# One-hot iota and residual tiles in a PSUM bank of VectorE's own, loads of the MLP loop in mid-turn, and a gather ring of 16 in the second layer

## The chip, the cores and the metric

The kernel runs on one core of a Trainium2 chip. The metric is device time in microseconds (us) of one execution. The core's engines work side by side and meet at semaphores: PE (TensorE, matmuls and transposes), DVE (VectorE), ACT (ScalarE), POOL (GpSimd, which here mostly issues gathers) and SP (which issues DMAs and passes on their landings).

## What is computed

Three blocks on a graph of 6250 nodes with 256 features and 100000 edges sorted by target:

```python
xn = layernorm(x)
# two SAGE layers: mean over incoming edges of gathered rows, two matmuls each
h   = relu(mean(xn[src] -> dst) @ W1l.T + b1 + xn @ W1r.T)
gnn =      mean(h[src]  -> dst) @ W2l.T + b2 + h @ W2r.T
# linear attention and an MLP with two layer norms
q, k, v = split(xn @ Wqkv.T);  q, k = elu(q) + 1, elu(k) + 1
t   = (q @ (k.T @ v)) / (q . sum(k) + eps)
x1  = LN(t + xn);  mix = LN(x1 + gelu(x1 @ W1.T + b1) @ W2.T + b2)
x   = x + gnn + mix
# experts: each row goes to the one of 8 with the largest gate
H   = gelu(layernorm(x) @ fW1 + fb1);  p = softmax(H @ Wg + bg)
out = x + p[best] * (H @ Wd[best] + bd[best])
```

## The kernel before

**Tiles and chunks.** Nodes are cut into 49 tiles of 128 rows, taken from the last rows to the first. Edges are cut into 197 superchunks (`SUPER`) of 4 x 128 edges, taken backwards too. Targets are skewed: late rows have few edges and early ones many, so the first tiles need 3 or 4 superchunks each and the last one 29. A pair of a superchunk and a tile is an item; there are 245 in a layer (`ITEMS`), read from a small table at run time.

**One item.** GpSimd issues four indirect DMAs (L699), each of which gathers 128 rows of 1 KB (a high and a low f16 half of each feature) into a slot of the ring `G`. SP waits for their landing and raises `s_ready` (`relay`, L604). VectorE builds a one-hot matrix `S` of 128 x 512 (`one_hot`, L898): it compares dst, less the tile's first row from `tv`, with an iota. PE multiplies `S` with the gathered rows and adds in the bank `AGG` (L1496; in layer 1 L1494 also counts the edges). `s_sum` counts items done. Before it fills a slot again GpSimd waits on `s_sum` for the last item of the chunk that lay there (L690 to L696). The ring has 8 slots in both layers, so GpSimd can be at most 8 chunks (32 gathers) ahead of PE.

**Layer 1** lasts through two loops of 49 turns. The mixer loop takes 3 items a turn and computes q, k, v of one tile and sums k.T v. The MLP loop takes 2 items a turn: attention output (`den`, `rc`, `tz`, `s`), layer norms, two matmuls with GELU. VectorE's order in a turn of the MLP loop i is written out: `from_stats(i)` with `rstds`, `n1` (L1049), `n2` (L1052), the two one-hots of the next turn, `res` (L1056); then `to_stats(i + 1)` with `st2` (L1007), `den` (L1015), `rc`, `tz` (L1020), `s` (L1026), `st1` (L1028). `m_t`, an SBUF tile, carries `tz` to `s` and `n2` to `res`. ScalarE's order (`turn_b`): `s2` (L1383), `x1T` (L1387), finish of a tile if the first item ended one, GELU (L1395), finish if the second did, then `next_loads`: it waits for `s` and `t` and issues the loads of x (L1368) and q (L1370) of the next tile. PE's order: `t` (L1593, needs q), transposes of n1, an item, w1, an item, w2 (L1615).

**Finish of a tile** (`finish1`), whenever its last item is summed: VectorE takes counts and mean (L914, L916), adds the residual of tile t-3 (L941), splits the hidden rows of t-2 in halves (L934, L936); PE runs `tr2` (t-2), `out1` (t-1) into bank `FO`, `r2` (t-2), `tr1` (t); ScalarE `meanT` (L1309, t-1), `hiddenT`, `relu` (t-1, out of `FO`), `xT_copy`, and stores h of t-2 to `hh_d`. `tr2` waits for `meanT`.

**Layer 2** starts its gathers from `hh_d` when all 49 tiles of h are stored. It has 5 items a turn; `finish2` adds the output (`out2` into `FO`, `x2` L1089), a layer norm, the hidden layer of 1024 and the gate logits. SP also loads the experts' weights `wd` (8 MB, 8 DMAs of 1 MB, L618) into `big`, which holds the transposed `xn` (`xnT`) in layer 1 and the ring at its end: six of them during layer 2, one every 24 chunks, the other two after the last sum. Then follow routing (L709, L1204, L1704) and the experts' matmuls (L1716 transposes, L1728), 56 slots.

## Time and profile before

| | us |
|---|---|
| median of 3 runs (2453.99 to 2458.47) | 2454.78 |
| the profiled execution | 2453.61 |
| its span, first to last instruction | 2451.8 |
| PE busy | 1925.4 (79%) |
| GpSimd busy | 1702.3 (69%) |
| VectorE busy | 1148.8 (47%) |
| ScalarE busy | 549.0 (22%) |
| mean granted TensorE clock | 0.891 of full speed |

A row of the costliest groups reads: line, engine, operation, output<-inputs by the program's names, shapes, count | busy us, mean ns of one | idle us of the engine just before them, with what ended most of it. Busy times of engines overlap, so they don't add up to the span. "issue" is time in which an engine waited for nothing that the profile shows. `bank` is any PSUM bank.

### The profile page before, as it was taken

How to read it: one execution, taken by the hardware profiler on the slowest of the kernel's cores; microseconds unless marked ns; L12 is line 12 of the kernel's file. 1: busy time of each engine (PE TensorE's matmuls, PEld its weight loads, DVE VectorE, ACT ScalarE, POOL GpSimd, SP SyncE). 2: the span in 40 equal slices, each digit the busy share in tenths (PEclk: the TensorE clock that was granted, in tenths of full speed). 3: DMA queues.
4: the chain of work that ended last, by engine and by line, in shares of the span. 5: the costliest groups of instructions: out<-in, count | busy, mean ns of one | idle time of the engine just before them, and what ended most of it. 6: DMA issues, size and time to landing. Idle time of an engine off the chain costs nothing.

```text
span 2451.8 us, 45561 instructions
## 1 busy us (share of the span) xinstructions
PE 1925.4 (79%) x9589; PEld 1190.2 (49%) x9590; DVE 1148.8 (47%) x3201; ACT 549.0 (22%) x1242; POOL 1702.3 (69%) x1773
## 2 busy tenths in 40 slices
PE   3799988878688887776899999877665543679998
PEld 2455555544455555543455555444332211368886
DVE  8544443433577777764555545433332221242221
ACT  6444333333222222221222222111100000101110
POOL 6777777777777777757777777777777777164442
PEclk9999999898899999997899999988776665689999
DMA  7444444444444444434454555444443333245551
GB/s 219 132 124 126 124 123 121 122 118 118 132 135 137 133 133 137 132 97 149 146 166 151 164 157 164 147 153 142 138 141 116 114 116 105 89 141 167 168 167 63
DMA packets 155000, 332.67 MB, mean 136 GB/s; under 512 B 34853, under 2 KB 89095, under 8 KB 154917
## 3 DMA queue, kind: packets, MB, share of 16 engines
q0 software_dynamic: 85824, 248.21, 34.6%
q10 hardware_dynamic: 42630, 58.35, 6.9%
q1 hardware_dynamic: 26466, 25.33, 3.4%
q14 instruction: 65, 0.53, 0.1%
q8 instruction: 15, 0.25, 0.0%
HBM read 273.97 MB, written 58.72 MB: 136 GB/s over the span
## 4 chain that ended last, share of the span: by engine, by line
PE 36%; POOL 33%; issue 15%; DVE 7%; DMA 4%; DVEq 2%; POOLq 2%; ACT 1%; ACTq 1%; SPq 0%
POOL big L699 32%; PE bank L538 12%; PE bank L1728 8%; PE bank L1496 6%; PE bank L1716 2%; PE bank L1502 2%; DMA mbuf<-qT_d 1%; PE bank L1526 1%; PE bank L1651 1%; PE bank L1521 1%; DMA big<-hh_d,edges 1%; POOL big L709 1%; POOLq L696 1%; DMA big<-xh_d,edges 1%; POOLq L694 1%
## 5 line engine op out<-in xcount | busy, mean ns | idle before, releaser
L699 POOL DMA_INDIRECT big<-xh_d,edges x782 | 769.8, 984 | 240.5 <-issue 232.4
L699 POOL DMA_INDIRECT big<-hh_d,edges x782 | 752.4, 962 | 261.1 <-issue 227.2
L1496 PE MATMUL bank<-big,S 128*128 x1960 | 589.0, 427 | 245.8 <-SPq L604 218.4
L898 DVE SCALAR_TENSOR_TENSOR S<-edges,tv,iota 128x512 f16<-128x512 f16 x490 | 368.6, 754 | 450.5 <-PE bank L1496 267.6
L1496 PEld LDWEIGHTS bank<-big,S 128*128 128x128 f16 x1960 | 203.7, 104 | 533.6 <-issue 389.8
L1494 PE MATMUL bank<-ones,S 128*128 128x1 f16 x980 | 165.4, 169 | 73.7 <-SPq L604 63.6
L538 PE MATMUL bank<-turned,x1T 128*128 128x512 f32 x392 | 195.6, 622 | 0.0
L720 POOL DMA_INDIRECT out_dram<-big,node_s x56 | 56.8, 1014 | 145.1 <-DVE big L1231 141.2
L1494 PEld LDWEIGHTS bank<-ones,S 128*128 128x128 f16 x980 | 95.5, 97 | 89.5 <-SPq L604 75.7
L1424 ACT ACTIVATE x1T<-bank 128x256 f32<-128x256 f32 x49 | 18.8, 383 | 531.7 <-PE bank L1502 531.7
L1231 DVE SCALAR_TENSOR_TENSOR big<-bank,prob_s,res 128x256 f32<-128x256 f32 x56 | 27.1, 484 | 179.4 <-PE bank L1730 179.4
L538 PEld LDWEIGHTS bank<-turned,abuf 128*128 128x128 f32 x784 | 96.6, 194 | 24.0 <-issue 22.9
L1438 ACT ACTIVATE mbuf<-bank 128x512 f32<-128x512 f32 x98 | 58.5, 597 | 205.0 <-PE bank L538 205.0
L1728 PE MATMUL bank<-big,mbuf 128*128 x448 | 101.4, 380 | 0.0
L1728 PE MATMUL bank<-big,abuf 128*128 x448 | 101.3, 379 | 0.0
L538 PEld LDWEIGHTS bank<-turned,x1T 128*128 128x128 f32 x392 | 66.9, 190 | 70.1 <-issue 70.1
L538 PE MATMUL bank<-turned,mbuf 128*128 128x512 f32 x196 | 95.2, 609 | 0.0
L914 DVE TENSOR_SCALAR lo<-bank,RC 128x256 f32<-128x256 f32 x98 | 47.4, 484 | 101.3 <-PE bank L1496 78.3
L538 PE MATMUL bank<-turned,abuf 128*128 128x8 f32 x784 | 92.1, 253 | 0.8 <-ACT abuf L1430 0.8
L1728 PEld LDWEIGHTS bank<-big,mbuf 128*128 128x128 f32 x448 | 83.0, 190 | 10.2
L1728 PEld LDWEIGHTS bank<-big,abuf 128*128 128x128 f32 x448 | 83.0, 190 | 10.1
L1593 PE MATMUL bank<-mbuf 128*128 128x132 f32 x196 | 36.7, 313 | 64.7 <-DMA mbuf<-qT_d 64.7
(228 smaller groups left out, 2910.4 us busy)
## 6 DMA issues: line engine op xcount, KB each, us to landing
hx_d<-mbuf ACTq DMA_DIRECT2D x49, 512.0 KB
big<-xh_d,edges POOLq DMA_INDIRECT x782
big<-hh_d,edges POOLq DMA_INDIRECT x782
big<-in_fwd_dram SPq DMA_DIRECT2D x8, 1024.0 KB, 6.4
qT_d<-abuf ACTq DMA_DIRECT2D x49, 128.0 KB
hh_d<-HL ACTq DMA_DIRECT2D x49, 128.0 KB
mbuf<-qT_d ACTq DMA_DIRECT2D x49, 128.0 KB, 2.6
hx_d<-res ACTq DMA_DIRECT2D x49, 128.0 KB
```

Of the source, the lines that this page charges most:

```text
L538: ins = eng.matmul(out_ap, a, b, start=(n == 0), stop=(n == len(pairs) - 1))
L699: e.indirect_dma_start(G[:, r, n % SC, :], None, table, bass.IndirectOffsetOnAxis(ap=srcx[:, n:n + 1], axis=0)).then_inc(d_g[r], 16)
L720: e.indirect_dma_start(out, bass.IndirectOffsetOnAxis(ap=node_s[:, i:i + 1], axis=0), o_sb[:, u, :], None, bounds_check=N - 1, oob_is_err= ...
L898: VI.done(e.scalar_tensor_tensor(S[:, walk.u, :, :], dst[:, bass.ds(c * SC, SC)].unsqueeze(2).to_broadcast([P, SC, P]), tv[:, bass.ds(k, 1 ...
L914: line.done(e.tensor_scalar(lo[:], AGG[:, C:2 * C], rc, None, ALU.mult), "lo")
L1438: AG2.done(e.activation(Hb[:, b * 512:b * 512 + 512], pb[4 + b][:], ACT.Gelu), f"g{b}")
L1494: e.matmul(CNT[:, 0:1], S[:, walk.u, j, :], ones16[:, 0:1], start=False, stop=False, skip_group_check=True)
L1496: ins = e.matmul(AGG[:], S[:, walk.u, j, :], G[:, bass.ds(slot, 1), j, :].rearrange("p a c -> p (a c)"), start=False, stop=False, skip_gro ...
L1502: ins = e.transpose(bank[:, off + h * P:off + (h + 1) * P], a[:, h * P:(h + 1) * P], ident[:])
L1593: ins = e.matmul(B4[:, h * (P + 4):(h + 1) * (P + 4)], qS[:, h, :], KVs[:, h, :], start=True, stop=True)
L1716: ins = e.transpose(((B4, B5), (FO, B7))[u % 2][b][:, q * P:(q + 1) * P], RB[:, u, (b * 4 + q) * P:(b * 4 + q + 1) * P], ident[:])
L1728: e.matmul(acc, (HT, HT2)[u % 2][:, j, :], wd[:, bass.ds(ex, 1), j, :].rearrange("p a c -> p (a c)"), start=(j == 0), stop=False)
```

## The change

1. The iota of the one-hots, an f16 tile in SBUF (`iota16`), becomes an f32 copy in the PSUM bank `FO` (`numbers_p`). `m_t` becomes `m_p` in the same bank for `tz`, `s`, `n2` and `res`. So that VectorE alone uses this bank in the two layers, `out1` goes to the upper half of bank `B5` (`FU`) and `out2` to the upper half of `FT` (`FV`). Two waits of PE are new: for `relu(t-1)` behind `tr1` in layer 1, and for `x2(t-1)` ahead of `tr1` in layer 2.
2. In the MLP loop ScalarE's `next_loads` moves from the end of the turn to behind `x1T`, ahead of the first finish and the GELU.
3. Layer 2 has a ring of 16 slots (`G2`), from the start of `big`, over what was `xnT`. Two memsets of GpSimd clear the unused parts of its first two chunks before it waits for `hh_d`. All eight expert loads now wait for the last sum, since `wd` lies where the ring is. `fbd` moves to `late`. The semaphores of slots 8 to 15 are shared with those of the experts' row gathers.

```diff
-RING = 8
+RING, RING2 = 8, 16
+RINGS = RING, RING2
@@
+        G2 = big[:, 0:RING2 * SC * C].bitcast(F16).rearrange("p (r j c) -> p r j c", r=RING2, j=SC)
+        GS = G, G2
-        iota16 = sb("iota16", [P, P], F16)
@@
-        fbd_f, fbd_t = big[0:3, 0:NE * C], w2r[0:3].rearrange("p h c -> p (h c)").bitcast(BF16)
+        fbd_f, fbd_t = late[0:3, 0:NE * C], w2r[0:3].rearrange("p h c -> p (h c)").bitcast(BF16)
@@
+        FU, FV = B5[:, C:2 * C], FT[:, C:2 * C]
+        numbers_p, m_p = FO[:, 0:P], FO[:, C:2 * C]
@@ SP
-            EVERY = SUPER // NE // PACK * PACK
-            SOON = XN // (HJ * C)
...
             for c in range(SUPER):
                 relay(1, c)
-                k, left = divmod(c + 1, EVERY)
-                if left == 0 and k <= SOON:
-                    if k == 1:
-                        e.wait_ge(s_fbd, 1)
-                    expert_rows(k - 1)
             e.wait_ge(s_sum, NS + 2 * ITEMS)
-            for k in range(SOON, NE):
-                expert_rows(k)
+            for k in range(NE):
+                e.dma_start(wd[:, k:k + 1, :, :].rearrange("p a j c -> p (a j) c"),
                             w["fwd"][k:k + 1].rearrange("a (j p) c -> p (a j) c", p=P)).then_inc(d_wd, 16)
@@ GpSimd
                 else:
+                    AX1.wait(e, "xT", TILES - 1)
+                    for c in range(2):
+                        e.memset(G2[:, ring(1, c), len(chunks(c)):, :].bitcast(F32), 0.0).then_inc(p_setup, 1)
                     e.wait_ge(d_h, 3 * OPENED + 16 * TILES)
...
-                    if c >= RING:
-                        n, left = divmod(c - RING, PACK)
+                    if c >= RINGS[layer]:
+                        n, left = divmod(c - RINGS[layer], PACK)
...
-                        e.indirect_dma_start(G[:, r, n % SC, :], None, table,
+                        e.indirect_dma_start(GS[layer][:, r, n % SC, :], None, table,
@@ VectorE
-            step(e.tensor_copy(iota16[:], ii[:, 0:P]))
...
+            step(e.tensor_copy(numbers_p, iof[:, 0:P]))
@@ one_hot
-                    tv[:, bass.ds(k, 1)], iota16[:].unsqueeze(1).to_broadcast([P, SC, P]),
+                    tv[:, bass.ds(k, 1)], numbers_p.unsqueeze(1).to_broadcast([P, SC, P]),
@@ s (tz writes m_p, n2 writes m_p, res reads m_p likewise)
-                step("s", at(lambda: e.scalar_tensor_tensor(m_s[:], xnS, rstd[:, bass.ds(raw(i), 1)], m_t[:], ALU.mult, ALU.add)))
+                step("s", at(lambda: e.scalar_tensor_tensor(m_s[:], xnS, rstd[:, bass.ds(raw(i), 1)], m_p, ALU.mult, ALU.add)))
@@ ScalarE, turn_b
                         AMB.done(e.activation(x1T[:, h, :], B5[:, h * P:(h + 1) * P], ACT.Identity, scale=lnT[:, h:h + 1],
                                               bias=lnT[:, CH + h:CH + h + 1]), f"x1T{h}")
+                if stage < 2:
+                    next_loads(i)
+                elif stage == 2:
+                    with e.If(i.base < TILES - 1):
+                        next_loads(i)
                 if stage <= 2:
                     walk = Ends(e, raw(i), 1, ITEMS_B, TILES * ITEMS_A)
                     finishes(walk, 1)
...
                 if stage <= 2:
                     finishes(walk, ITEMS_B - 1)
-                if stage < 2:
-                    next_loads(i)
-                elif stage == 2:
-                    with e.If(i.base < TILES - 1):
-                        next_loads(i)
@@ PE, finish1 and finish2
                     PT1.done(transposes(FT, 0, mean), "tr1")
+                    AR1.wait(e, "relu", t, 1)
...
                     clear(AGG[:])
+                    VX2.wait(e, "x2", t, 1)
                     PT2.done(transposes(FT, 0, mean), "tr1")
```

## Rows read from the trace of the kernel before

**Rows 1.** The page's chain that ended last, shares of the span by line
```profile
POOL big L699 32%; PE bank L538 12%; PE bank L1728 8%; PE bank L1496 6%; PE bank L1716 2%; PE bank L1502 2%; DMA mbuf<-qT_d 1%; PE bank L1526 1%; PE bank L1651 1%; PE bank L1521 1%; DMA big<-hh_d,edges 1%; POOL big L709 1%; POOLq L696 1%; DMA big<-xh_d,edges 1%; POOLq L694 1%
```
**Rows 2.** The page's costliest groups: gathers of both layers, one-hots
```profile
L699 POOL DMA_INDIRECT big<-xh_d,edges x782 | 769.8, 984 | 240.5 <-issue 232.4
L699 POOL DMA_INDIRECT big<-hh_d,edges x782 | 752.4, 962 | 261.1 <-issue 227.2
...
L898 DVE SCALAR_TENSOR_TENSOR S<-edges,tv,iota 128x512 f16<-128x512 f16 x490 | 368.6, 754 | 450.5 <-PE bank L1496 267.6
```
**Rows 3.** Instructions of L699, layer 1: ns min/median/max, first and last start us
```profile
L699 POOL DMA_INDIRECT big<-xh_d,edges x782: 942/946/1472, 75.5 to 1082.3; - x196
```
**Rows 4.** Timeline 192 to 197: start us, us, engine line op tiles [idle before <-releaser]
```profile
192.16 0.95 POOL L699 DMA_INDIRECT big<-xh_d,edges  x1 [0.30 <-issue]
196.06 1.39 POOL L699 DMA_INDIRECT big<-xh_d,edges  x1 [0.30 <-issue]
...
192.13 0.48 DVE L916 SCALAR_TENSOR_TENSOR mean<-bank,RC,lo 128x256 f32<-128x256 f32 x1
195.10 1.53 DVE L898 SCALAR_TENSOR_TENSOR S<-edges,tv,iota 128x512 f16<-128x512 f16 x2 [1.42 <-issue]
```
**Rows 5.** Timeline, the first and the last of the 153 long gathers inside one-hots
```profile
82.00 1.16 POOL L699 DMA_INDIRECT big<-xh_d,edges  x1 [0.30 <-issue]
...
1975.81 0.96 POOL L699 DMA_INDIRECT big<-hh_d,edges  x1 [0.30 <-issue]
```
**Rows 6.** VectorE's waits, 660 to 1064 us: us in total, times, longest
```profile
DVE mbuf L1015 <- PE bank L1593: 4.3, 8, 1.1
```
**Rows 7.** Timeline 717 to 731, an MLP turn whose first item ends a tile
```profile
717.34 0.41 DVE L1049 TENSOR_SCALAR mbuf<-m_s,lnt 128x256 f32<-128x256 f32 x1
...
719.44 0.38 ACT L1309 ACTIVATE mT<-bank 128x256 f32<-128x256 f32 x1
...
722.04 0.48 DVE L1026 SCALAR_TENSOR_TENSOR m_s<-mbuf,rstd,m_t 128x256 f32<-128x256 f32 x1 [0.24 <-DVE m_t L1020]
...
728.09 0.41 DVE L1049 TENSOR_SCALAR mbuf<-m_s,lnt 128x256 f32<-128x256 f32 x1
...
728.51 0.35 ACTq L1368 DMA_DIRECT2D mbuf<-in_x_dram  x1
729.04 0.34 ACTq L1370 DMA_DIRECT2D mbuf<-qT_d  x1
...
730.43 0.38 ACT L1383 ACTIVATE mbuf<-bank 128x256 f32<-128x256 f32 x1 [2.07 <-PE bank L1615]
```
**Rows 8.** PE's waits, 652 to 1090 us
```profile
PE bank L1593 <- DMA mbuf<-qT_d: 57.7, 45, 2.4
PE bank L1494 <- SPq L604: 13.1, 7, 2.8
```
**Rows 9.** GpSimd's waits, 1100 to 2100 us
```profile
POOL big L699 <- DMA hh_d<-HL: 17.9, 1, 17.9
POOL big L699 <- PE bank L1496: 16.0, 35, 2.2
```
**Rows 10.** PE's waits, 1530 to 2100 us
```profile
PE bank L1496 <- SPq L604: 217.2, 78, 5.5
```
**Rows 11.** VectorE's groups by form, whole span
```profile
L914 DVE TENSOR_SCALAR lo<-bank,RC 128x256 f32<-128x256 f32 x98 | 47.4, 484 | 101.3 <-PE bank L1496 78.3 <-issue 21.3
...
L1049 DVE TENSOR_SCALAR mbuf<-m_s,lnt 128x256 f32<-128x256 f32 x49 | 20.6, 421 | 1.8
...
L1205 DVE TENSOR_TENSOR S<-iof,mx 128x512 f32<-128x512 f32 x3 | 2.8, 949 | 0.0
```
**Rows 12.** DMA issues (KB each, median us to landing); timelines of SP and PE behind layer 2
```profile
big<-in_fwd_dram SPq DMA_DIRECT2D x8, 1024.0 KB, 6.4
...
2100.73 0.99 SPq L618 DMA_DIRECT2D big<-in_fwd_dram  x2
...
2175.07 1.30 PE L1716 MATMUL bank<-ident,res 128*128 128x128 f32 x5 [7.13 <-DMA res<-hx_d,node_g]
```

More of the change, by code:

```diff
@@ L415, in build @@
         s_perm, s_fbd = sem("s_perm"), sem("s_fbd")
-        d_rb = [sem(f"d_rb{u}") for u in range(RB_SLOTS)]
+        assert RING2 - RING == RB_SLOTS
+        d_rb = d_g[RING:]
+        RB_BASE = [16 * sum(len(chunks(c)) for c in range(SUPER) if ring(1, c) == RING + u) for u in range(RB_SLOTS)]
         d_out = [sem(f"d_out{u}") for u in range(OB_SLOTS)]
@@ L539, in matmuls @@
             return ins
-        def chunks(c):
-            first = (SUPER - 1 - c) * SC
-            return range(min(first, CHUNKS), min(first + SC, CHUNKS))
-        def ring(layer, c):
-            return (layer * SUPER + 1 + c) % RING
         def landed(layer, c):
@@ L1687, in _ @@
             e.wait_ge(d_w2, X_IN + 16 * 3)
+            e.wait_ge(p_setup, 3 + 8 + 2)
             with e.Fori(0, TILES) as i:
```

42 lines of the change are left out of this document (23 added, 19 removed).

## The prediction

> **What bounds the kernel.** I read the chain of work that ended last first: GpSimd's gather, L699, is its longest line, 32% of the span [rows 1]. The costliest groups say what kind of 32% that is: 782 gathers per layer, a mean of 984 ns in the first and 962 ns in the second, with 0.30 us of issue before each and almost no other wait [rows 2]. So each layer is a train of gathers at 1.25 us, and matmuls, mixer and MLP run beside it. In layer 1 the train runs from 75.5 to 1083 us, in layer 2 from 1101 to 2097 us; what lies between is the last tiles' tail, and behind it come routing and expert matmuls, which the change leaves alone but for one load.
>
> The second look is at one gather. The least and the median are 942 and 946 ns, the longest 1472 [rows 3], so something lengthens some of them. The timeline shows it [rows 4]: the gather of 196.06 began inside a one-hot (L898, two of 0.75 us from 195.10 to 196.63) and took 1.39 us, ending 0.82 us after the one-hot, as if it had begun at 196.5. The gather of 192.16 began inside L916, just as long an instruction, and took its 0.95. L898 reads two tensors from SBUF (dst and the iota), L916 one from SBUF and one from PSUM. I counted along the timeline the gathers over 0.962 us that begin while an L898 is under way: 75 in layer 1 with 19.7 us over 0.942, 78 in layer 2 with 10.6 us (the first and the last are [rows 5]). L1026, with two SBUF tensors too, costs another 0.9 us; of 67 gathers that begin well inside L914, L916, L941 or L1089 (an input in PSUM) none exceeds 0.96. The whole excess is busy time less 0.942 us a gather [rows 2, 3]: 769.8 - 782 x 0.942 = 33.2 us in layer 1 and 752.4 - 736.6 = 15.8 in layer 2; L898 and L1026 are 31.2 of these 49.
>
> The Trainium skill, SBUF — State Buffer, § Who interferes with whom, has the rule: a VectorE instruction with two SBUF inputs contends with a GpSimd instruction that reads SBUF, one with a single SBUF input does not. By it the whole 31.2 us goes. The same page says that whoever starts second blocks, VectorE too; no row here shows that half.
>
> **Who else is close to the bound.** In layer 1 the mixer loop keeps meeting the gathers, so what they gain there arrives. The MLP loop (49 turns from 652 us) is VectorE's own serial chain: it waits for PE only 4.3 us in 404 [rows 6], its turns measure 8.4 us, and 10.75 where a tile ends (L1049 at 717.34 and 728.09, [rows 7]). It falls behind the gathers and catches up only in the last tile: PE waits for chunks 13.1 us in this stretch, nearly all near its end [rows 8]. That 13.1 is the MLP loop's margin. In layer 2 PE lags between 1165 and 1550 us; there the ring of 8 fills and GpSimd waits [rows 9]. After 1530 PE waits 217 us for chunks [rows 10], so a lag of PE is made good.
>
> **The change, part by part.**
> (1) Iota in PSUM. 245 one-hots a layer no longer read two SBUF tensors. GpSimd gains 19.7 + 0.9 us in layer 1 (13.0 in the mixer loop, 7.6 in the MLP loop) and 10.6 in layer 2. L1026 and L1056 go the same way with their m_p operand; L1052, L936, L963 and L966 keep two SBUF tensors, and their hits (some 9 us) stay. The price of the one-hot itself: no row has this form. The bounds are 0.06 us below 754 ns (484 less 421, the step between one-input instructions with and without PSUM, taken downwards) and a 128x512 f32 comparison of two SBUF tensors at 949 ns [rows 11]; near in form is L916, 0.48 us with an input in PSUM [rows 4], against 0.48 for L1026 out of SBUF [rows 7]. I take 754 as it is, so 0 in the sum; the range keeps -0.06 and +0.20 us each. L1020 now writes PSUM, which no row shows; I bound it by the same 0.06 either way.
> (2) Loads in mid-turn. ScalarE now waits for VectorE's s (L1026) ahead of the finish of a tile and the GELU, and issues two DMAs there, both with their address steps: 1.0 us, from just ahead of L1368 at 728.51 to the end of L1370 at 729.38 [rows 7]. Plain turns: s ends 5.2 us into the turn, the GELU slips from about 4.5 to 6.2, w2 ends at about 8.9 and s2 needs n2 at 9.2 anyway: no cost. Turns that end a tile at their first item, 7 of them (tiles 39, 40, 41, 43, 45, 46, 47; the turn of 717 is [rows 7]): meanT moves from 719.44 to behind s and the loads, 722.52 + 1.1 = 723.6. PE's tr2, out1 and r2 wait for it and end 1.8 us later; s2 of the next turn moves from 730.43 to 732.2, its stats from 731.02 to 732.65. Part of that was lost already to the late q, so 1.0 us each is new. The two tiles that end at the second item cost 0.25. Sum 7.5 us in the MLP loop. The gain is q, for which PE waits 57.7 us [rows 8]; but VectorE, which sets the loop, is held by it only 4.3, and w2 is as late. No gain; the range keeps -4.3.
> (3) Ring of 16. GpSimd's waits for PE in layer 2 are 16.0 us in 35, of which 35 x 0.3 is the usual issue: 5.5 us go [rows 9], and faster gathers would otherwise have filled 8 slots sooner.
> (4) Expert weights. Six 1 MB loads move from layer 2 behind the last sum at 2101; before, two were there. PE needs them at 2175, 74 us later. One takes 6.4 us from issue to landing, in the median, beside gathers [rows 12]; eight in a row are 51: hidden by routing. If not, each us beyond 74 is paid.
> (5) Added waits. PE waits for relu(t-1) behind tr1; by the timeline relu ended 0.6 to 1.9 us before PE's next step in 47 of 48 tiles, 0.1 in the first: free; queued behind it are the next item's matmuls. PE's wait for x2(t-1) ahead of tr1 has hidden and logits between: x2 ended 5 us or more earlier in all but the first four tiles. GpSimd's two memsets lie in the 17.9 us in which it waits for hh. h and o in other banks cost nothing.
>
> Layer 1: the gathers gain 20.6. The MLP loop's margin of 13.1 shrinks by its 7.6 to 5.5, its turns grow by 7.5, so 2.0 come back: -18.6. Layer 2: 10.6 + 5.5 = -16.1. Sum -34.7; I round to -34 because not every wait of PE is margin of VectorE. The profiled execution took 2453.61 us (span 2451.8), 1.2 under the median of 2454.78: 2419.6 in its terms, **2421** against the median.
>
> **Rivals.**
> A. PSUM operands cost VectorE some 65 ns each. For it: 484 against 421 ns in one-input instructions [rows 11]; against it: 0.48 and 0.48 us in two-input ones [rows 4, 7]. Per MLP turn two one-hots and two m_p readers, 0.26 us x 49 = 12.7 us, all beyond the margin: layer 1 gains 5.9, layer 2 its 16.1: 2433. The Trainium skill, VectorE: DVE Perf Modes, § The TRN2 errata, has this as a rule (120 cycles fixed out of PSUM against 58 out of SBUF).
> B. No relief: the pointer scalar tv and dst in SBUF still hold the gather up. Against it L916, which has both kinds. Layer 1 then gains 0 (7.5 fit into 13.1), layer 2 its 5.5: 2449.
> C. Slower: the one-hot itself gets long, at 490 places, and the MLP loop pays two a turn. It decides from 34.7 / 49 = 0.71 us a turn, 0.35 a one-hot, so 1.1 us instead of 0.75. At 949 ns (the upper row) layer 1 gains nothing and the time is 2440; at half rate (754 ns for 512 columns and 484 for 256 make 270 per 256, so 540 more) the turn grows by 1.08, 53 us, and the time is 2473.
>
> **How the numbers follow.** The forecast holds with 0.60 (2413 to 2430: the q gain and -0.06 below, some growth above), A 0.15, the upper row of C 0.05, B 0.13, C slower 0.07. The range 2412 to 2446 takes in the first three. 0.2%, 4.9 us, is about what a measurement of this kernel tells from no change: faster 0.83, same 0.10 (B with a little growth), slower 0.07.
>
> **What would show it.** (1) L699's mean falls from 984 to about 957 ns in layer 1 and from 962 to about 948 in layer 2, and no gather that begins in a one-hot is long; L898 stays at 754. (2) MLP turns stay at 8.4; those behind a tile's end grow by about 1 us; waits for q are gone. (3) GpSimd's waits for PE in layer 2 are zero. (4) The first expert matmul comes as long after the last sum as before. Wrong would be: long gathers still inside one-hots (B), L898 over 0.8 us (A, C), or a GpSimd that waits for PE in the MLP loop by more than some us, which says that VectorE's chain has taken over layer 1.

## The result, and the profile after

The changed kernel takes 2445.11 us (median of 5 runs, 2444.01 to 2446.76) against 2458.47 us before (5 runs): a ratio of 0.9951, 95% interval 0.9939 to 0.9964, 12 to 13 us faster (the ratios here and below compare all runs of both kernels and differ from the quotient of the medians by up to 0.0006). Forecast were 2421 us, 34 faster than the 2454.78 us known then. The direction was right, and most of the gain did not arrive. The time still lies just inside the stated range of 2412 to 2446 us; 7 us of it, the end of the kernel below, are luck.

Of the page of the changed kernel, first the gathers of both layers and the one-hot, the lines that answer to [rows 2]; columns are busy us, mean ns | idle before and its releaser:

```profile
L699 POOL DMA_INDIRECT big<-xh_d,edges x782 | 746.1, 954 | 270.5 <-issue 229.4
L699 POOL DMA_INDIRECT big<-hh_d,edges x782 | 741.6, 948 | 246.1 <-issue 232.7
...
L898 DVE SCALAR_TENSOR_TENSOR S<-edges,tv,bank 128x512 f16<-128x512 f32 x490 | 365.5, 747 | 472.3 <-PE bank L1496 287.9
```

The gathers lost what they were to lose: over 0.942 us each they keep 746.1 - 736.6 = 9.5 us in layer 1 (33.2 before) and 5.0 in layer 2 (15.8), and the one-hot costs 747 ns instead of 754. Counted by the starts in the two traces, 133 gathers of layer 1 and 154 of layer 2 begin inside a one-hot, and none of them takes over 0.962 us; in the kernel before, counted in the same way, 74 of 129 and 74 of 162 did. But the idle time before the gathers of layer 1 rose from 240.5 to 270.5 us. GpSimd's waits from 640 to 1100 us (us, times, longest) show what they wait for:

```profile
POOL big L699 <- issue: 95.0, 312, 0.3
POOL big L699 <- PE bank L1496: 36.7, 22, 8.1
```

The single waits of up to 8.1 us for TensorE's sums did not exist before (five of 0.3 us in this stretch). The MLP loop's turns have become too long, its ring of 8 is full, and the gathers stand still. The instructions of L699 and of the turn's L1049 (min/median/max ns, first and last start) give the stretches; first the changed kernel, then the kernel before:

```profile
L699 POOL DMA_INDIRECT big<-xh_d,edges x782: 940/946/1188, 75.7 to 1088.8; - x196
L699 POOL DMA_INDIRECT big<-hh_d,edges x782: 942/946/1718, 1113.0 to 2091.5; - x196
...
L1049 DVE TENSOR_SCALAR mbuf<-m_s,lnt x49: 411/414/639, 640.7 to 1104.7; 128x256 f32<-128x256 f32 x49
```

```profile
L699 POOL DMA_INDIRECT big<-hh_d,edges x782: 940/946/1721, 1101.1 to 2095.8; - x196
...
L1049 DVE TENSOR_SCALAR mbuf<-m_s,lnt x49: 411/412/635, 652.2 to 1091.1; 128x256 f32<-128x256 f32 x49
```

The MLP loop begins 11.5 us earlier (640.7 against 652.2), because the mixer loop got its part of the gain, and ends 13.6 later: it grew from 438.9 to 464.0 us. Layer 2's train starts 11.9 us later and is 16.2 shorter (978.5 against 994.7).

The last piece is the very end. VectorE's last instruction and the span, before (first) and after:

```profile
span 2451.8 us, 45561 instructions
...
2440.06 0.48 DVE L1231 SCALAR_TENSOR_TENSOR big<-bank,prob_s,res 128x256 f32<-128x256 f32 x1 [3.19 <-PE bank L1730]
```

```profile
span 2442.6 us, 45582 instructions
...
2437.90 0.48 DVE L1231 SCALAR_TENSOR_TENSOR big<-bank,prob_s,res 128x256 f32<-128x256 f32 x1 [3.19 <-PE bank L1733]
```

Behind the last result come the last scatter and a drain on GpSimd: 11.2 us before, 4.2 after. So 7.0 of the profile's 9.2 us (2451.8 to 2442.6) lie where no step of the prediction looked; the work itself ended 2.2 us earlier. (The medians are 13.4 us apart, since the profiled execution of the kernel before was a quick one, 2453.61 against 2458.47 us; the stretches below divide the 9.2.)

The same stretches of every kernel whose comparison bears on this, each read in the same way from the one profiled execution of its kernel (a train is counted from first to last start, "rest" is from layer 2's last gather to VectorE's last result):

| kernel | median us, before beside it | ratio (95%) | layer 1 | to layer 2 | layer 2 | rest | closing | MLP loop |
|---|---|---|---|---|---|---|---|---|
| before | 2458.5 | | 1006.8 | 18.8 | 994.7 | 344.7 | 11.2 | 438.9 |
| after | 2445.1, 2458.5 | 0.9951 (0.9939-0.9964) | 1013.1 | 24.2 | 978.5 | 346.9 | 4.2 | 464.0 |
| e1b: loads back at the end | 2412.0, 2457.4 | 0.9809 (0.9793-0.9826) | 985.5 | 20.9 | 980.1 | 343.6 | 4.2 | 433.6 |
| e3c: PSUM part alone | 2434.5, 2457.1 | 0.9913 (0.9896-0.9929) | 985.3 | 17.9 | 994.1 | 346.5 | 11.2 | 430.9 |
| e4d: ring part alone | 2443.9, 2456.6 | 0.9951 (0.9935-0.9968) | 1009.7 | 20.4 | 986.1 | 344.4 | 4.2 | 439.4 |
| e8c: q in mid-turn, x at the end | 2410.4, 2459.0 | 0.9808 (0.9789-0.9827) | 986.2 | 19.0 | 978.2 | 346.7 | 4.2 | 430.3 |

How far such stretches scatter can be seen in e4d, whose layer 1 is that of the kernel before and took 2.9 us longer; "rest" goes from 343.6 to 346.9 us, in no order with what was changed. Differences below some 3 us in one stretch say nothing by themselves, the closing one excepted, which is the same to 0.1 us in all of them.

### The profile page after: what moved, and what is told of

The parts are those of the page before. It is cut to its first block, busy times and chain, and to the rows that moved or that the text cites. A ratio compares the mean times of both kernels' runs of the same rounds, so it can differ in the third digit from the quotient of the medians.

```text
span 2442.6 us, 45582 instructions
## 1 busy us (share of the span) xinstructions
PE 1926.5 (79%) x9589; PEld 1194.5 (49%) x9590; DVE 1151.4 (47%) x3201; ACT 549.3 (22%) x1242; POOL 1669.2 (68%) x1775
## 4 chain that ended last, share of the span: by engine, by line
PE 36%; POOL 29%; issue 15%; DVE 11%; DVEq 3%; DMA 2%; ACT 2%; POOLq 1%; ACTq 1%; SPq 0%
POOL big L699 28%; PE bank L554 11%; PE bank L1731 8%; PE bank L1496 6%; PE bank L1719 2%; PE bank L1502 2%; PE bank L1526 2%; PE bank L1521 1%; PE bank L1616 1%; DVEq L488 1%; PE bank L1652 1%; DVE m_s L1026 1%; DVE bank L1020 1%; POOL big L709 1%; POOLq L696 1%
## 5 line engine op out<-in xcount | busy, mean ns | idle before, releaser
L699 POOL DMA_INDIRECT big<-xh_d,edges x782 | 746.1, 954 | 270.5 <-issue 229.4
L699 POOL DMA_INDIRECT big<-hh_d,edges x782 | 741.6, 948 | 246.1 <-issue 232.7
L1496 PE MATMUL bank<-big,S 128*128 x1960 | 583.6, 424 | 231.6 <-SPq L611 213.6
L898 DVE SCALAR_TENSOR_TENSOR S<-edges,tv,bank 128x512 f16<-128x512 f32 x490 | 365.5, 747 | 472.3 <-PE bank L1496 287.9
L1496 PEld LDWEIGHTS bank<-big,S 128*128 128x128 f16 x1960 | 203.5, 104 | 516.7 <-issue 376.3
L1494 PE MATMUL bank<-ones,S 128*128 128x1 f16 x980 | 166.1, 169 | 36.6 <-SPq L611 35.9
L1424 ACT ACTIVATE x1T<-bank 128x256 f32<-128x256 f32 x49 | 18.8, 383 | 516.1 <-PE bank L1502 516.1
L1494 PEld LDWEIGHTS bank<-ones,S 128*128 128x128 f16 x980 | 96.1, 98 | 43.6 <-SPq L611 40.7
L1616 PE MATMUL bank<-turned,mbuf 128*128 128x256 f32 x196 | 57.2, 416 | 73.9 <-ACT mbuf L1400 73.8
L914 DVE TENSOR_SCALAR lo<-bank,RC 128x256 f32<-128x256 f32 x98 | 47.4, 484 | 93.5 <-PE bank L1496 67.6
## 6 DMA issues: line engine op xcount, KB each, us to landing
big<-in_fwd_dram SPq DMA_DIRECT2D x8, 1024.0 KB, 13.3
```

Of the source, the lines that this page charges most:

```text
L699: e.indirect_dma_start(GS[layer][:, r, n % SC, :], None, table, bass.IndirectOffsetOnAxis(ap=srcx[:, n:n + 1], axis=0)).then_inc(d_g[r], 16)
L898: VI.done(e.scalar_tensor_tensor(S[:, walk.u, :, :], dst[:, bass.ds(c * SC, SC)].unsqueeze(2).to_broadcast([P, SC, P]), tv[:, bass.ds(k, 1 ...
L1494: e.matmul(CNT[:, 0:1], S[:, walk.u, j, :], ones16[:, 0:1], start=False, stop=False, skip_group_check=True)
L1496: ins = e.matmul(AGG[:], S[:, walk.u, j, :], GS[layer][:, bass.ds(slot, 1), j, :].rearrange("p a c -> p (a c)"), start=False, stop=False, ...
L1616: ins = e.matmul(o, a, b, start=(n == 0), stop=(n == len(out2) - 1), skip_group_check=True)
```

## The experiments

Theory T: the mid-turn loads cost the MLP loop far more than was priced. Its rivals: VectorE's work in PSUM makes the turns longer, or the MLP loop has a limit of its own, on which the gathers' gain is lost anyway.

**The loads back at the turn's end.** Edit to the changed kernel:

```diff
-                if stage < 2:
-                    next_loads(i)
-                elif stage == 2:
-                    ...
                 if stage <= 2:
                     walk = Ends(e, raw(i), 1, ITEMS_B, TILES * ITEMS_A)
                     finishes(walk, 1)
...
                     finishes(walk, ITEMS_B - 1)
+                if stage < 2:
+                    next_loads(i)
+                elif stage == 2:
+                    ...
```

> [...] On a chip on which the kernel before takes about 2456 us, theory T (the mid-turn loads cost some 25 us of the MLP loop) gives 2415 to 2427 us, and the loop from first to last n1 near 439 us; rivals R and P (the loads are harmless, or the gain is only handed on) give 2435 to 2449. [...]

2412.0 us, ratio 0.9809: 33.1 us under the changed kernel, 3.0 us below T's window of 2415 to 2427, so T's direction and more than its size, and far from the rivals'. Its rows, gathers and L1049:

```profile
L699 POOL DMA_INDIRECT big<-xh_d,edges x782: 940/946/1198, 75.8 to 1061.3; - x196
L699 POOL DMA_INDIRECT big<-hh_d,edges x782: 942/946/1720, 1082.2 to 2062.3; - x196
...
L1049 DVE TENSOR_SCALAR mbuf<-m_s,lnt x49: 411/413/640, 640.3 to 1073.9; 128x256 f32<-128x256 f32 x49
```

The MLP loop takes 433.6 us, though VectorE works in PSUM here too. So the loads' place is the cause, by 30.4 us of loop. This is shown beside the other two parts; the loads alone in the kernel before (e2, e2b) never ran where the kernel before takes 2457 us, so it is not shown that they would cost as much without the PSUM bank and its added waits. Counted by the starts of L1049, 27.9 of these lie in seven turns, each of them the turn behind one whose first item ends a tile: 12.2 to 13.6 us in the changed kernel, 8.4 to 10.0 here. One of them in the timelines (start us, us). First the changed kernel, steps of VectorE, ScalarE and TensorE (the turn with the finish starts at L1049, 861.58):

```profile
866.27 0.48 DVE L1026 SCALAR_TENSOR_TENSOR m_s<-mbuf,rstd,bank 128x256 f32<-128x256 f32 x1 [0.24 <-DVE bank L1020]
...
867.05 0.34 ACTq L1368 DMA_DIRECT2D mbuf<-in_x_dram  x1
867.57 0.34 ACTq L1370 DMA_DIRECT2D mbuf<-qT_d  x1
868.92 0.38 ACT L1309 ACTIVATE mT<-bank 128x256 f32<-128x256 f32 x1 [4.46 <-issue]
...
869.45 0.66 PE L1502 MATMUL bank<-ident,hb 128*128 128x128 f32 x2 [4.58 <-ACT mT L1309]
...
876.95 0.62 ACT L1400 ACTIVATE mbuf<-bank,turned 128x128 f32<-128x128 f32 x2 [2.08 <-PE bank L554]
...
878.14 0.75 DVE L898 SCALAR_TENSOR_TENSOR S<-edges,tv,bank 128x512 f16<-128x512 f32 x1 [3.94 <-PE bank L1496]
...
879.65 0.38 ACT L1383 ACTIVATE mbuf<-bank 128x256 f32<-128x256 f32 x1 [2.07 <-PE bank L1616]
```

and with the loads at the end (the same turn starts at 843.71):

```profile
846.01 0.38 ACT L1309 ACTIVATE mT<-bank 128x256 f32<-128x256 f32 x1 [0.19 <-issue]
...
847.65 0.63 PE L1502 MATMUL bank<-ident,hb 128*128 128x128 f32 x2
...
854.09 0.62 ACT L1395 ACTIVATE mbuf<-bank,turned 128x128 f32<-128x128 f32 x2 [1.54 <-PE bank L554]
854.87 0.35 ACTq L1368 DMA_DIRECT2D mbuf<-in_x_dram  x1
...
856.78 0.38 ACT L1383 ACTIVATE mbuf<-bank 128x256 f32<-128x256 f32 x1 [2.07 <-PE bank L1616]
```

Measured from the turn's L1049, meanT (L1309) moves from +2.3 to +7.3 us, TensorE's transpose of it (L1502) from +3.9 to +7.9, the GELU from +10.4 to +15.4 and s2 (L1383) from +13.1 to +18.1. Between the second load's issue (over at 867.91) and meanT another 1.0 us passes in which ScalarE's sequencer does the register steps of the finish, 867.93 to 868.87. In the kernel before, in the turn of 717, the same steps run from 718.45 on, while ScalarE is busy with x1T. TensorE's wait for meanT (L1309), 640 to 1080 us, in the changed kernel and with the loads at the end:

```profile
PE bank L1502 <- ACT mT L1309: 28.6, 9, 4.6
```

```profile
PE bank L1502 <- ACT mT L1309: 0.9, 2, 0.5
```

VectorE is caught from two sides: its second one-hot waits 3.94 us for a sum of TensorE that stands behind the late steps, and the stats of s2 come behind it.

TensorE also works at the lower of its two levels for longer. Stretches of both kernels (busy and count of PE, PEld, DVE, ACT, POOL; then the granted clock), first the changed kernel, then the loads at the end:

```profile
867.70:869.40 1.70, 0.00 (x0) 0.00 (x0) 1.63 (x5) 0.38 (x1) 1.31 (x2) 0.50 0.64 224
869.45:874.40 4.95, 4.95 (x13) 3.45 (x14) 3.46 (x14) 0.60 (x2) 2.44 (x3) 0.50 0.37 107
```

```profile
845.90:849.30 3.40, 3.40 (x12) 2.24 (x13) 2.91 (x10) 0.77 (x2) 2.60 (x3) 0.50 0.41 116
849.30:851.00 1.70, 1.68 (x7) 0.77 (x5) 1.50 (x6) 0.00 (x0) 1.27 (x2) 1.00 0.25 77
```

In the changed kernel the clock falls to 0.50 at 867.6, within the wait that began at 864.9, and is back at 1.00 at 874.5. With the loads at the end it falls too, at 845.9, behind waits of 1.64 and 0.74 us, and is back at 849.3. At 0.50 (1.2 GHz) throughout, the matmuls from L1521 to L1526 take 4.25 us; at 0.50 and then 1.00 (2.4 GHz) they take 2.9.

**Which step of the loads?** The wait for s, or the issue itself? The loads are taken apart: q waits only for t, which is done about a microsecond into the turn, and x waits for s.

```diff
+            def load_q(i):
+                PMt.wait(e, "t", i - 1)
+                q = i * P if isinstance(i, int) else within(e, raw(i), TILES - 1) * P
+                e.dma_start(qS, qT_d[bass.ds(q, P), :]...).then_inc(d_lq, 16)
...
                 VD.wait(e, "s", i)
-                PMt.wait(e, "t", i)
-                load_b(i + 1)
+                load_x(i + 1)
...
                 if stage < 2:
-                    next_loads(i)
+                    load_q(i + 1)
...
                     finishes(walk, ITEMS_B - 1)
+                if stage < 2:
+                    next_loads(i)
```

> The changed kernel with the two loads taken apart, for a chip on which the kernel before takes about 2457 us: q in mid-turn, where it waits for t alone, x at the turn's end, where it waits for s. Theory T (the wait for s ahead of the finish part and the GELU is what costs): 2408 to 2420 us, against 2412.0 with both at the end and 2445.1 with both in mid-turn. Rival M (the DMA issue itself ahead of the table load, or the transfers in mid-turn, cost): 2425 to 2440.

2410.4 us, ratio 0.9808: theory T. q's DMA issue ahead of the finish costs nothing that shows (in the turn that starts at 844.34 meanT stands at +2.6 us); the wait for s is what costs, with x's issue behind it, 0.5 us in the timeline above, which this run does not tell apart from the wait. The run shows a second thing. TensorE's waits from 640 to 1080 us, with the loads at the end (first) and with q in mid-turn (L1507 and L1509 there are L1494 and L1496, L1515 the transposes of L1502):

```profile
PE bank L1594 <- DMA mbuf<-qT_d: 62.9, 48, 2.5
PE bank L1494 <- DVE S L898: 11.8, 22, 1.1
```

```profile
PE bank L1507 <- DVE S L898: 43.7, 41, 1.8
PE bank L1515 <- DVE mbuf L1049: 26.2, 23, 1.5
```

The 62.9 us for q are gone, and 58.1 us more for two results of VectorE have come. The loop is 3.3 us shorter (430.3), and the time the same within the interval (2412.0 and 2410.4). So what TensorE no longer waits for q, it waits for VectorE.

A third place, both loads behind the GELU and ahead of the second finish part, was meant for the same question:

> The changed kernel with the same two loads issued a step later: behind the GELU and ahead of the second finish part, so that the first finish part, its table load and the GELU come before the wait for s. Theory T (what costs is that the ScalarE steps on which TensorE waits stand behind the wait for s and two DMA issues): nearly all of the 33 us come back, 2412 to 2418 us, and q still arrives earlier than with the loads at the turn's end. Rival M (what costs is q and x arriving early, or two transfers in mid-turn beside the gathers): it stays at 2435 to 2445.

It ran only where the kernel before takes 3130 to 3200 us (below), which tells nothing: inconclusive.

**The PSUM part alone**, in the kernel before: iota and m_p in the bank, h and o moved, the two added waits.

```diff
-                    tv[:, bass.ds(k, 1)], iota16[:].unsqueeze(1).to_broadcast([P, SC, P]),
+                    tv[:, bass.ds(k, 1)], numbers_p.unsqueeze(1).to_broadcast([P, SC, P]),
...
+                    AR1.wait(e, "relu", t, 1)
...
+                    VX2.wait(e, "x2", t, 1)
```

> The kernel before with the iota and the turn's temporary in the PSUM bank, the moved results and the two added waits; on a chip on which the kernel before takes about 2457 us. Theory T: -20.6 us in the first layer and -10.6 in the second, as in the prediction's sum: 2426 us (2422 to 2430). The kernel with this part and the ring took 2412.0 us. Rival R (VectorE's work in PSUM costs the MLP loop's turns): 2440 to 2450. On a chip on which the kernel before takes over 3000 us it came out 1.7% slower (3184 against 3135), which decides nothing for the chip of the result.

2434.5 us, ratio 0.9913: 22.6 us faster, between T's window and the rival's. The gathers of both layers on its page, their instructions, and GpSimd's wait in the second layer:

```profile
L700 POOL DMA_INDIRECT big<-hh_d,edges x782 | 741.6, 948 | 270.3 <-issue 229.7
L700 POOL DMA_INDIRECT big<-xh_d,edges x782 | 748.3, 957 | 240.5 <-issue 233.6
```

```profile
L700 POOL DMA_INDIRECT big<-xh_d,edges x782: 942/946/1197, 75.5 to 1060.8; - x196
L700 POOL DMA_INDIRECT big<-hh_d,edges x782: 941/946/1718, 1078.7 to 2072.8; - x196
```

```profile
POOL big L700 <- PE bank L1497: 23.7, 28, 3.3
```

Layer 1's train is 985.3 us, 21.5 shorter: all of the relief (33.2 to 11.7 over 0.942) arrives, and the MLP loop is 8.0 us shorter as well, so VectorE's turns don't suffer from PSUM. Layer 2's is 994.1 against 994.7: nothing. Its gathers lost 10.8 us of lengthening (15.8 to 5.0) and GpSimd's waits for TensorE rose from 16.0 us in 35 [rows 9] to 23.7 in 28; less 0.3 us of usual issue each, from 5.5 to 15.3. The ring of 8 hands the gain on as waiting, though not all of this waiting is the ring's: all waits lie in the first 270 us of the train, where GpSimd is held by TensorE, and there TensorE itself runs late. Its 241st matmul of L1497 in layer 2 comes 251.4 us behind the first gather, against 247.0 in the kernel before, and the 241st gather 317.9 against 313.8. What makes TensorE 4 us later in this run was not found. The rest of the train takes 676.2 us against 680.9, so the shorter gathers do pay there.

**The ring part alone**: the changed kernel without the other two parts, so with `RING2 = 16` and the experts' table loaded behind the last sum.

> The changed kernel without its other two parts: ring of 16 in the second layer, experts' table loaded behind the last sum; on a chip on which the kernel before takes about 2457 us. Theory X (with the ring of 8 the second layer's gathers are held by waits for TensorE, so shorter gathers only turn into waits there, and parts 1 and 3 are needed together): here the waits go, 5 to 8 us, the gathers stay as long as before, and 2457 - 7 (drain) - 6 + 3 (experts' phase) gives 2445 to 2449. Rival A (the ring is worth 14 us in the gathers whatever their length): 2436 to 2440. The rest of the story does not hang on it.

2443.9 us, ratio 0.9951: 12.7 us faster, 1.1 below X's window and 3.9 above A's: X had the waits right, and took the gathers' lengthening as unchanged, which it is not. Its rows:

```profile
L698 POOL DMA_INDIRECT big<-hh_d,edges x782 | 749.2, 958 | 246.9 <-issue 232.7
```

```profile
L698 POOL DMA_INDIRECT big<-xh_d,edges x782: 942/946/1472, 75.6 to 1085.3; - x196
L698 POOL DMA_INDIRECT big<-hh_d,edges x782: 942/946/1719, 1105.7 to 2091.8; - x196
```

```profile
POOL big L698 <- PE bank L1495: 5.2, 17, 0.3
```

Layer 2's train is 8.6 us shorter: the 5.4 us of waits are gone (5.2 us in 17 is the usual 0.3), and fewer gathers met a one-hot: 58 long ones among the 138 that begin in one, where there were 74 among 162, and 12.6 us over 0.942 in all instead of 15.8. Nothing was changed in the gathers themselves; it is another timing. Add lengthening and waits beyond 0.3 and take them from the train: 994.7 - 15.8 - 5.5 = 973.4 before, 994.1 - 5.0 - 15.3 = 973.8 for part 1, 986.1 - 12.6 - 0.1 = 973.4 for part 3, 978.5 - 5.0 - 0.1 = 973.4 for the changed kernel. The train is nothing else. Parts 1 and 3 gave 0.6 and 8.6 alone, and 16.2 together in the changed kernel (14.6 in e1b and 16.5 in e8c, which have both too); the first pays here only under the second.

**The closing drain.** All kernels with the ring part have 4.2 us from VectorE's last result to the end, all without it 11.2. This run moves the six early loads of the experts' table behind the last sum, in the kernel before (with them goes SP's wait for `fbd`), and nothing else:

```diff
             for c in range(SUPER):
                 relay(1, c)
-                k, left = divmod(c + 1, EVERY)
-                ...
             e.wait_ge(s_sum, NS + 2 * ITEMS)
-            for k in range(SOON, NE):
+            for k in range(NE):
```

> The kernel before with one edit: the eight loads of the experts' table, six of which were issued along the second layer, are all issued behind the last sum; ring, iota and MLP loads as before. It asks two things. First the closing drain: from the last result of VectorE to the span's end the kernels without the ring part take 11.2 us, those with it 4.2. Theory D (an expert load's place makes it): 4.2 us here. Rival E (the shared semaphores of the ring and the gather slots, or the memsets in the second layer): 11.2 us here, and the place of the loads is not it. This can be read on any chip. Second the loads' price: the traces say the experts' phase loses 2 to 3 us by them and the prediction said nothing: between 2454 and 2460 us with theory E, 7 less with D, on a chip on which the kernel before takes about 2457 us.

```profile
span 3149.8 us, 45561 instructions
...
3138.04 0.48 DVE L1221 SCALAR_TENSOR_TENSOR big<-bank,prob_s,res 128x256 f32<-128x256 f32 x1 [3.18 <-PE bank L1720]
```

11.2 us (3138.52 to 3149.8): theory E, the place of the loads is not it. What is left of the part was not told apart: the larger ring, two memsets on GpSimd, the place of `fbd`, and the semaphores that the gathered rows of the experts share with the ring. A kernel with eight semaphores of their own for the rows (e9) needs more semaphores than are free and gave no result, so the cause stays open. The price of the late loads shows in the "rest" of the table: 344.4, 343.6, 346.7 and 346.9 us with them, 344.7 and 346.5 without. It doesn't hang on them.

**Runs at over 3100 us.** Thirteen runs of the same kernels, and the run of the experts' loads above, fell where the kernel before itself takes 3130 to 3205 us. The expectations take this for a matter of the chip, but one chip number gave both times: with chip 14 the kernel before took 2457.4 us beside e1b and 3205.1 beside e4c. No difference of these runs enters the argument, but they are results. The ratios to the kernel before were 1.014 (1.008-1.020) for the loads at the end, 1.005 and 1.009 for the mid-turn loads alone, 1.018 and 1.017 for the PSUM part alone, 1.000, 1.000 and 1.002 for the ring part alone, 1.021, 1.013 and 1.011 for the loads behind the GELU, 1.013 and 1.015 for q alone in mid-turn, and 1.004 for the experts' loads. The expectations:

> The changed kernel with one part undone: q and x of the next tile are issued at the turn's end again; the iota in PSUM and the ring of 16 stay. Theory T (the loads in mid-turn are what was priced too low: the traces show the MLP loop's 49 turns 25.2 us longer, 438.8 to 464.0 us from the first n1 to the last, about 4 us of it in each of the seven turns that follow a turn with a finish as its first item): the loop shrinks by some 25 us, the first layer's gathers end near 1065 us instead of 1089.7, and the time is 2445 - 25 = about 2420 us (2415 to 2427), a ratio to the kernel before of 0.984. Rival R (the loads are harmless where they stand; the MLP loop is longer because tz, s, n2 and res of VectorE's turn now go through the PSUM bank, or because its ring of 8 is full anyway, so that earlier gathers only wait): the loop stays above 455 us, the time is within 4 us of 2445. Rival P (the gathers' gain in the mixer's loop is only handed on as waiting, since the MLP loop has a margin of its own that VectorE's chain sets): the loop shrinks but POOL waits for TensorE instead, time 2435 to 2445.

> The kernel before with one part of the change: q and x of the MLP loop's next tile issued in mid-turn, ahead of the finish work and the GELU. Theory T: the MLP loop is some 20 to 25 us longer than in the kernel before; it had a margin of 13.1 us against the gathers, and POOL's wait for TensorE appears in the loop, so the time is 7 to 15 us longer, 2465 to 2474 us (ratio 1.003 to 1.006). The step on record (7.5 us for this part) would stay under the margin: 2458, no change. Rival R (harmless loads): 2458, loop at 439 us.

> The kernel before with one part of the change: q and x of the MLP loop's next tile issued in mid-turn. Undoing this part in the changed kernel gave 2412.0 us instead of 2445.1, so the part costs 33 us there. Theory T (it lengthens the MLP loop itself): the loop from first to last n1 goes from 438.8 to 455 to 465 us. The gathers of this loop then end later by that less their margin of 13.1 us: 2465 to 2474 us. Rival I (the part hurts only together with the PSUM bank, for instance by the two added waits): within 4 us of 2457. The step on record (7.5 us, under the margin) gives 2457 as well, but with a loop of 446 us.

> The kernel before with one part of the change: the iota and the temporary of the turn in the PSUM bank, the two matmul results moved to other banks, and the two waits that this adds. Theory T: the gathers lose 20 to 24 us of their lengthening in the first layer and 10 in the second, and the MLP loop keeps its turns of 9.07 us, so the time is 2458 - 20 - 10 = about 2428 us (2422 to 2434), ratio 0.988. Rival R (VectorE's operands in PSUM make the turns of the MLP loop longer, which is what the changed kernel shows): the loop is above 455 us and the time about 2450. Also read: the length of the closing drain on GpSimd, 10.4 us in the kernel before and 3.4 in the changed one.

> The kernel before with the iota and the turn's temporary in the PSUM bank, the moved results and the two added waits. Theory T: -20.6 us in the first layer and -10.6 in the second, as in the prediction's sum: 2457 - 31 = 2426 us (2422 to 2430). With the ring's 5.5 us on top this is the 2412 to 2421 that the changed kernel gives without its mid-turn loads. Rival R (VectorE's work in PSUM costs the MLP loop's turns): 2440 to 2450.

> The changed kernel without its other two parts: only the ring of 16 in the second layer, with the experts' table loaded behind the last sum. Theory T: POOL's waits for TensorE and for hh in the second layer (16.0 and 17.9 us) shrink by some 10 us together, less 2 us that the experts' phase loses by the late loads, less what the memset adds: 2450 to 2456 us. The step on record said -5.5 us for the ring and nothing for the loads: 2453. Rival R (the loads of the experts behind the last sum cost what the ring gives, or more): 2457 to 2465. Also read: whether the closing drain is 3.4 us here, which would make it the work of the loads' place.

> The kernel before with the ring of 16 and the experts' table loaded behind the last sum. The step on record: -5.5 us, 2452. From the traces: POOL's waits in the second layer, 17.9 us for hh and 16.0 for TensorE, were 13.7 + 8.2 us and 5.2 in the changed kernel, which is 6.8 us less, and the experts' phase lost 2.2 us: 2452 to 2453. Rival (the last gathers' order decides, not their sum): 2457. The closing drain on GpSimd is expected at 3.4 us here and at 10.4 in the other kernels that load experts early, if it hangs on the loads' place; if it varies from run to run, it is neither.

> The changed kernel without its other two parts: ring of 16 in the second layer, experts' table loaded behind the last sum; on a chip on which the kernel before takes about 2457 us. With the PSUM part under it, this part was worth 22.4 us (2434.5 to 2412.0): 14.1 in the second layer's gathers, 7.0 in the closing drain, the rest around them. Theory X (the second layer's gathers with the ring of 8 are held by waits for TensorE, so the PSUM part's shorter gathers only turn into waits there and both are needed together): here the waits go, 5 to 8 us, but the gathers stay as long as before, so 2457 - 7 (drain) - 6 + 3 (experts' phase) = 2445 to 2449. Rival A (the ring is worth 14 us in the gathers whatever their length): 2436 to 2440.

> The changed kernel with the same two loads issued a step later: behind the GELU and ahead of the second finish part, so that the first finish part, its table load and the GELU come before the wait for s. The loads at the turn's end gave 2412.0 us, in mid-turn ahead of the finish part 2445.1. Theory T (what costs is that the ScalarE steps on which TensorE waits stand behind the wait for s and two DMA issues): nearly all of the 33 us come back, 2412 to 2418 us. Rival M (what costs is q and x arriving early, or two transfers in mid-turn beside the gathers): it stays at 2435 to 2445. On a chip on which the kernel before takes over 3000 us neither can be told.

> The changed kernel with the two loads behind the GELU and ahead of the second finish part, on a chip on which the kernel before takes about 2457 us. At the turn's end they gave 2412.0 us, in mid-turn ahead of the first finish part 2445.1. Theory T (what costs is that the first finish part, its table load and the GELU stand behind the wait for s and two DMA issues): 2412 to 2418 us. Rival M (what costs is q and x arriving early, or two transfers in mid-turn): 2435 to 2445. In between, 2420 to 2432, would say that the second finish part, now the one behind the wait, matters nearly as much as the first.

> The changed kernel with the two loads taken apart: q in mid-turn, where it waits for t alone (done about a microsecond into the turn), x at the turn's end, where it waits for s. Theory T (the wait for s ahead of the finish part and the GELU is what costs): 2412 to 2420 us, as with both at the end (2412.0), less what q's earlier arrival gives: TensorE waited 70 us for q in the loop there and 10 with the loads in mid-turn. If that wait is on the path, the time falls below 2410; if not, it stays at 2412. Rival M (the DMA issue itself in mid-turn, which stands before the table load, or the transfers, cost): 2425 to 2440. On a chip on which the kernel before takes over 3000 us nothing can be told from its time.

> The changed kernel with the two loads taken apart, again, for a chip on which the kernel before takes about 2457 us: q in mid-turn, where it waits for t alone, x at the turn's end, where it waits for s. Theory T (the wait for s ahead of the finish part and the GELU is what costs): 2408 to 2420 us, against 2412.0 with both at the end and 2445.1 with both in mid-turn. Rival M (the DMA issue itself ahead of the table load, or the transfers in mid-turn, cost): 2425 to 2440.

None of the theories can be read there, since the gathers are not the bound. The page of the ring part alone, and one place in the timeline of the mid-turn loads alone:

```profile
L698 POOL DMA_INDIRECT big<-xh_d,edges x782 | 763.1, 976 | 683.6 <-PE bank L1495 373.0
```

```profile
236.57 0.16 DVE L925 TENSOR_SCALAR cntv<-bank 128x1 f32<-128x1 f32 x1 [11.23 <-issue]
237.30 0.38 ACT L1313 ACTIVATE hT<-bank 128x256 f32<-128x256 f32 x1 [11.09 <-remote]
```

A gather takes 976 ns here and 988 in the same kernel at 2444 us, so GpSimd's instructions are not longer. VectorE and ScalarE idle for 11.2 and 11.1 us, 9.4 of them together, with nothing in the profile that releases them. TensorE's mean granted clock is 0.79 instead of 0.89 and its busy time 2119 us instead of 1928, and GpSimd waits for it, 373 us in layer 1. What lies behind this is open. That every kernel with the PSUM part is 1.1 to 2.1% slower there, where it is faster at 2457 us, is measured and not explained.

## Why the prediction was right in direction and wrong in size

(1) **Iota in PSUM: right in layer 1, right in layer 2 only through the ring.** Forecast were 20.6 us less lengthening in layer 1 and 10.6 in layer 2; the part alone takes away 21.5 and 10.8. That L898 would stay at 754 ns held (747). L1020, now writing PSUM, went from 425 to 433 ns. Rival A's 65 ns are there for one-input instructions (L914 484 against 421, [rows 11]) and not for those whose second input lies in SBUF: L1026 481 ns with an operand in PSUM, 485 without. VectorE's groups by form, in the kernel before (first) and in the changed one:

```profile
L1026 DVE SCALAR_TENSOR_TENSOR m_s<-mbuf,rstd,m_t 128x256 f32<-128x256 f32 x49 | 23.8, 485 | 11.3 <-DVE m_t L1020 11.0 <-issue 0.2
```

```profile
L1026 DVE SCALAR_TENSOR_TENSOR m_s<-mbuf,rstd,bank 128x256 f32<-128x256 f32 x49 | 23.6, 481 | 11.3 <-DVE bank L1020 11.2
...
L1020 DVE TENSOR_TENSOR bank<-bank,mbuf 128x256 f32<-128x256 f32 x49 | 21.2, 433 | 1.7
```

The Trainium skill, VectorE: DVE Perf Modes, § The TRN2 errata, gives 120 cycles of fixed cost out of PSUM against 58 out of SBUF and names no form; the trace agrees for L914 and not for L1026. Of the Trainium skill, SBUF — State Buffer, § Who interferes with whom, the half that GpSimd is relieved when VectorE reads only one tensor from SBUF agrees with the trace: none of the 287 gathers that begin in a one-hot is long. The other half, that whoever starts second blocks, was left open by the prediction, and the trace of the kernel before speaks against it for this pair of instructions: 404 of its 490 one-hots begin inside a gather, and none of these takes over 755 ns.

(2) **Loads in mid-turn: the step that failed.** It was priced at 7.5 us in the MLP loop, 1.0 for each of seven turns; measured are 30.4 us of loop, some 4.0 for each of the seven, and 33.1 us in the time. The mechanism was named rightly (meanT behind s and the loads, then everything on TensorE behind meanT), and its size was lost in three places. meanT was put at +6.3 us of the turn and stands at +7.3, since the finish's register steps, which ran under x1T before, now stand open behind the loads. Its effect on TensorE was put at 1.8 us; before, tr2 started 3.8 us into the turn (721.12, against 717.34 in [rows 7]), now 7.9, which is 4.1. Even by the forecast's own meanT, 723.6 and 0.38 us long, tr2 could not have begun before 724.0, 2.9 us later. And TensorE's work behind it, at a granted clock of 0.50 for longer, adds about 1.3. And "part of that was lost already to the late q, so 1.0 each is new" had no row: s2 moved from 13.1 to 18.1 us behind the turn's start, 5.0, of which 4.0 stayed in the turns. The forecast also looked at s2 alone; VectorE's second one-hot waits for TensorE's sums as well (26.8 us in 8 waits in the loop, 10.6 in 5 with the loads at the end). TensorE's tr2 in the turn of [rows 7], in the kernel before; then VectorE's wait in the changed kernel, 640 to 1110 us:

```profile
721.12 0.41 PE L1502 MATMUL bank<-ident,hb 128*128 128x128 f32 x2 [0.46 <-issue]
```

```profile
DVE S L898 <- PE bank L1496: 26.8, 8, 4.4
```

"No gain from q" was right, and for the reason given: taking the 62.9 us of waits away changed the time by no more than the interval.

(3) **Ring of 16: sum right, division wrong.** Forecast 5.5 us, alone 8.6 in the train, 5.4 by the waits and 3.2 by fewer long gathers. With part 1 the two were to give 16.1 in layer 2, and gave 16.2. The clause "faster gathers would otherwise have filled 8 slots sooner" was true; but part 1's 10.6 are credited to part 1 in the sum, though it gives 0.6 without the ring. That the sum came out to 0.1 us is partly luck: the other two kernels with both parts gave 14.6 and 16.5.

(4) **Experts' loads: right.** Hidden: they were put at 51 us in a row, and the last of the eight lands 30.5 us behind the first issue (2096.4 to 2126.9), though each takes 13.3 us in the median where 6.4 [rows 12] was taken. They overlap. The first transpose of the experts (L1719) comes 73.7 us behind the last sum, 74.4 before, and TensorE waits for no load of the weights; the rest of the kernel stays within 343.6 to 346.9 us with and without.

(5) **Added waits: right in layer 1**, by e3c, whose MLP loop with them is shorter than before. In layer 2 TensorE waits 0.2 us once for x2 from 1110 to 1560 us in e3c, so the added wait is not seen to cost there either. The memsets are hidden as put: behind them GpSimd still waits 8.2 us for hh.

**Not in the prediction**: the closing drain, -7.0 us. Without it the changed kernel would have been about 6 us faster than before, at some 2452 us, outside the range. That the range holds is luck. The sum by stretches: layer 1 with the step to layer 2 was to give -18.6 and gave +11.7 (6.3 + 5.4), layer 2 -16.1 and -16.2, the rest 0 and +2.2, the closing 0 and -7.0; together -34.7 forecast and -9.3 by the table, against -9.2 by the spans.

The warning that the prediction wrote down, a GpSimd that waits for TensorE in the MLP loop by more than some us, is the line that appeared. The version without the faulty part, 2412.0 us, and the one with q alone in mid-turn, 2410.4, beat both kernels.

## What to carry to other kernels

When a load is moved up in an engine's program, its wait moves with it: price every step that now stands behind that wait, on the engine and on the engines that wait for it. Take the start of the other engine's work from its own row, and don't write off a part of the delay as lost already without a row that shows it. Split a pair of loads by what each waits for before moving either. A long row of waits for a transfer (62.9 us here) is no gain in sight as long as the engine that sets the loop is not among the waiters. And where a producer fills a ring, shorten its steps and look at its waits for the consumer together: one without the other gave 0.6 and 8.6 us, both gave 14.6 to 16.5.

## What the hardware showed that was not expected

- A gather that begins inside a one-hot with both tensors in SBUF takes up to 1.47 us instead of 0.94; with one of them in PSUM none of 287 takes over 0.962. The one-hot itself takes 755 ns at most when it begins inside a gather.
- In a wait of 4.58 us TensorE's granted clock fell to 0.50, the lower of its two levels (1.2 GHz), and stayed there through the first 5.0 us of work behind the wait, 869.45 to 874.4. With the loads at the end, where it had worked on items instead, it was at 0.50 from 845.9 to 849.3. The matmuls from L1521 to L1526 took 4.25 us against 2.9.
- The end of the kernel costs 11.2 or 4.2 us behind the last result, the same to 0.1 us in all kernels of a kind, at 2457 and at over 3100 us, by something in the ring part other than the place of the experts' loads.
- Eight 1 MB loads issued in a row land in a median of 13.3 us each, all within 30.5 us; six spread along the gathers and two at the end took 6.4 [rows 12]. The changed kernel's line of DMA issues:

```profile
big<-in_fwd_dram SPq DMA_DIRECT2D x8, 1024.0 KB, 13.3
```

- The same program takes 2457 us at some times and 3130 to 3205 at others, and one chip number gave both. GpSimd's instructions are not longer there; TensorE's mean granted clock is 0.79 instead of 0.89, and VectorE and ScalarE idle together for 9.4 us in the one place shown. The cause is open.
